# Two-layer graph kernel, one core: adj times h0 before W_g, scores in the wide product, 512-column E pieces, loops written out

## The reference, cut to what matters

```python
h0 = maximum(layernorm(x), 0)                        # x: 2048 x 256
h  = h0 @ W_sa;  s_left = h @ a_l;  s_right = h @ a_r
e  = where(adj != 0, exp(-leaky_relu(s_left[:, None] + s_right[None, :], 0.01)), 0)
x_a = (e / (sum(e, axis=1) + 1e-5)) @ h              # adj: 2048 x 2048, zeros and ones
x_b = adj @ (h0 @ W_g) + b_g
gate_a = sigmoid([adj @ h0, h0] @ Wa.T + ba);  gate_b = sigmoid([adj @ h0, h0] @ Wb.T + bb)
out = x + sigmoid(gate_a * x_a + gate_b * x_b)
```

## Time and profile before

| | us |
|---|---|
| median of 3 runs (190.56 to 190.69) | 190.69 |
| span of the profiled execution, first to last instruction | 189.2 |
| outside the span (the difference) | 1.5 |
| PE, DVE, ACT, POOL busy | 175.0, 154.3, 117.3, 37.1 |

### The profile page before, as it was taken

One profiled execution on the slowest core, in us unless ns is written; L12 is line 12 of the kernel. 1 busy time (PEld: TensorE's weight loads), 2 busy tenths in 40 slices (PEclk: granted clock), 3 DMA queues, 4 the chain that ended last, 5 costly groups with the idle time before them and its releaser, 6 DMA issues.

```text
span 189.2 us, 4431 instructions
## 1 busy us (share of the span) xinstructions
PE 175.0 (92%) x1576; PEld 144.4 (76%) x1576; DVE 154.3 (82%) x389; ACT 117.3 (62%) x231; POOL 37.1 (20%) x86
## 2 busy tenths in 40 slices
PE   0359899999999999999999999999999999999993
PEld 0335465466888888888888888888888888888892
DVE  0698789999999989996997898599869896997341
ACT  2197586899647958664696458466727764594310
POOL 1057770099970010002000200020020000000000
DMA  5920797000029008311901470175109210001100
GB/s 141 396 102 0 110 185 155 2 3 0 0 28 196 2 5 155 67 59 16 196 15 55 63 158 6 49 120 102 55 0 178 43 55 0 0 0 55 61 28 28
DMA packets 4621, 13.67 MB, mean 72 GB/s; under 512 B 512, under 2 KB 896, under 8 KB 4608
## 3 DMA queue, kind: packets, MB, share of 16 engines
q0 software_dynamic: 2304, 8.39, 24.8%
q1 hardware_dynamic: 2016, 4.20, 6.2%
q10 hardware_dynamic: 288, 0.92, 1.3%
HBM read 19.80 MB, written 2.10 MB: 116 GB/s over the span
## 4 chain that ended last, share of the span: by engine, by line
PE 80%; DVE 3%; issue 0%; ACT 0%; DVEq 0%
PE ps L800 15%; PE ps L801 15%; PE ps L807 14%; PE ps L808 14%; PE ps L806 14%; PE ps L765 4%; PE ps L838 1%; PE ps L837 1%; PE ps L836 1%; DVE mv_lo L603 1%; PE ps L756 1%; DVE h0t_lo L581 1%; DVE mv_lo L601 1%; PE ps L745 0%; DVE e_raw L342 0%; DVE far L333 0%
## 5 line engine op out<-in xcount | busy, mean ns | idle before, releaser
L349 ACT ACTIVATE e_raw<-e_raw,log_e 128x512 f32<-128x512 f32 x64 | 46.1, 720 | 43.9 <-DVE e_raw L342 43.1
L806 PE MATMUL ps<-mv_lo,e_hi 128*128 128x257 f16 x240 | 65.5, 273 | 0.0
L808 PE MATMUL ps<-mv_hi,e_lo 128*128 128x257 f16 x240 | 65.5, 273 | 0.0
L807 PE MATMUL ps<-mv_hi,e_hi 128*128 128x257 f16 x240 | 65.4, 272 | 0.0
L342 DVE SCALAR_TENSOR_TENSOR e_raw<-sl_row,exs,far 128x256 f32<-128x256 f16 (+1 forms) x128 | 56.6, 482 | 2.5 <-DVE far L333 2.0
L801 PE MATMUL ps<-mv_lo,adj 128*128 128x258 f16 x256 | 56.9, 272 | 0.0
L800 PE MATMUL ps<-mv_hi,adj 128*128 128x258 f16 x256 | 56.9, 273 | 0.0
L360 DVE TENSOR_TENSOR e_lo<-e_raw,e_hi 128x512 f16<-128x512 f32 x64 | 44.5, 697 | 3.8 <-ACT e_hi L356 3.8
L356 ACT ACTIVATE e_hi<-e_raw 128x512 f16<-128x512 f32 x64 | 39.3, 616 | 0.0
L800 PEld LDWEIGHTS ps<-mv_hi,adj 128*128 128x128 f16 x256 | 24.7, 96 | 3.8 <-ACT sl_row L471 0.2
L801 PEld LDWEIGHTS ps<-mv_lo,adj 128*128 128x128 f16 x256 | 24.8, 97 | 3.3
(11 more groups left out here) (80 smaller groups left out, 179.9 us busy)
## 6 DMA issues: line engine op xcount, KB each, us to landing
adj<-in_adj_t POOLq DMA_DIRECT2D x16, 512.0 KB, 7.1
x_sb<-in_x SPq DMA_DIRECT2D x4, 512.0 KB, 8.0
out<-res SPq DMA_DIRECT2D x7, 256.0 KB, 2.0
w_sb<-in_weights ACTq DMA_DIRECT2D x1, 512.0 KB, 8.1
c_sb<-in_consts ACTq DMA_DIRECT2D x1, 391.0 KB, 5.7
out<-res SPq DMA_DIRECT2D x1, 128.0 KB, 1.8
out<-res SPq DMA_DIRECT2D x2, 64.0 KB, 1.6
```

The costliest lines, as they stand in the source:

```text
L349: act.activation(e_raw[:, p % RING, :, :], e_raw[:, p % RING, :, :], ACT.Exp, bias=log_e[:, 0:1], scale=SLOPE - 1.0).then_inc(exp_done, 1)
L806: pe.matmul(a_bank(s, q), e_hi[:, j, cols], mv_lo[:, j, 0, 0:D + 1], start=(j == 0), stop=False)
L807: pe.matmul(a_bank(s, q), e_hi[:, j, cols], mv_hi[:, j, 0, 0:D + 1], start=False, stop=False)
L808: return pe.matmul(a_bank(s, q), e_lo[:, j, cols], mv_hi[:, j, 0, 0:D + 1], start=False, stop=(j == NT - 1))
```

## The change

- adj is no longer multiplied with h0 W_g, but with h0 itself: `b_products` (stationary the natural-layout parts nat_hi, nat_lo of h0, moving adj16 at 512 columns, two 128-row halves k of the result) gives the aggregate, transposed. `agg_highs` and `agg_lows` split it, and `post` multiplies it with W_g and the left gate vectors (258 columns, 6 matmuls a tile). There are now 4 chunks (c) of 512 rows, and 8 pairs of tiles (p).
- `narrow` is gone. The scores and the right gate vectors stand beside W_sa: `wide` has 260 columns.
- relu comes before the transpose (`h0_tiles`), and h0 is split twice: as it stands (`nat_highs`, `nat_lows`) and transposed (`h0t_highs`, `h0t_lows`). The transposes have one set of banks (0, 1), which `sl_rows` also writes; so `turn(g)` waits for the copy `sl_rows(g-2)` on ACT. `wide(g)` has four banks and waits for `mv_lows(g-1)`.
- The reciprocal square root is one pow on POOL; the Newton steps are gone.
- E comes in 32 pieces (n) of two adj tiles by 512 columns, all of them after the head, with a ring of 12 pieces for PE (ESLOT). Pair p waits for `a_side(p-2)` on DVE (a_read).
- adj has three slots, is loaded from the landing of x's second part on, in 9 loads. The weights' load waits for x's first part. The half that is added to x is now added on ACT.
- All engine programs are written out, without loops.

The core of the diff:

```diff
-CW = 256
+CW = 512
+ZRING = 3
+ESLOT = 12
+ADJ = 3
+WA = D + NX
+WG = D + 2
+WIDE_BANKS = (2, 3, 6, 7)
+B_BANKS = (4, 6, 4, 4)
+ADJ_PIECES = ((0, 0, 4), (0, 4, 8), (0, 8, 16), (1, 0, 8), (1, 8, 16), (2, 0, 8), (2, 8, 16), (3, 0, 8), (3, 8, 16))
...
         def _(pool):
-            def correct(g):
...
+            def norms(g):
+                ts = slice(g * GT, (g + 1) * GT)
+                pool.wait_ge(var_ready, g + 1)
+                pool.tensor_tensor(rstd[:, ts], var_s[:, ts], power[:, :], ALU.pow).then_inc(rstd_ready, 1)
+                pool.wait_ge(rstd_ready, g + 1)
+                pool.tensor_tensor(shift[:, ts], neg_mean[:, ts], rstd[:, ts], ALU.mult).then_inc(norm_ready, 1)
...
+            pool.wait_ge(x_landed[1], 16)
+            load_adj(0)
+            norms(0)
+            load_adj(1)
+            norms(1)
+            load_adj(2)
+            load_adj(3)
+            norms(2)
+            load_adj(4)
+            scales(0)
...
+            pool.wait_ge(b_done, 1)
+            pool.wait_ge(far_ready, JP)
+            load_adj(7)
+            load_adj(8)
...
         def _(act):
             act.dma_start(c_sb[:, :], consts).then_inc(c_landed, 16)
-            act.dma_start(w_sb[:, :, :, :], weights).then_inc(w_landed, 16)
+            act.wait_ge(x_landed[0], 16)
+            act.dma_start(w_sb[:, :, :], weights).then_inc(w_landed, 16)
...
+            h0_tiles(0)
             act.wait_ge(wl_product, 1)
             act.wait_ge(w_landed, 16)
+            act.activation(w_sb[:, :, D:D + 2], wl_bank, ACT.Copy).then_inc(wl_ready, 1)
+            act.wait_ge(wl_ready, 1)
+            act.activation(w_hi[:, :, 0:WA], w_sb[:, :, 0:WA], ACT.Copy, scale=W_SCALE).then_inc(w_high, 1)
+            h0t_highs(0)
+            nat_highs(0)
+            h0_tiles(1)
+            h0t_highs(1)
+            nat_highs(1)
             factors(0)
+            h0_tiles(2)
+            mv_highs(0)
+            sl_rows(0)
+            h0t_highs(2)
+            nat_highs(2)
+            factors(1)
+            h0_tiles(3)
+            mv_highs(1)
+            sl_rows(1)
+            h0t_highs(3)
...
+            def dve_far(n):
...
+                dve.tensor_scalar(far[:, n % 2, :, :], adj16[:, c % ADJ, j:j + 2, :], -FAR, FAR, ALU.mult, ALU.add)\
+            def dve_z(n):
...
+                if n >= ZRING:
+                    dve.wait_ge(e_ready, n - ZRING + 1)
...
+            dve_far(0)
+            for n in range(NE):
+                if n + 1 < NE:
+                    dve_far(n + 1)
+                dve_z(n)
+                if n >= LAG:
+                    dve_low(n - LAG)
...
+                if n == 20:
+                    agg_lows(3)
+                for p in range(2, 6):
+                    if n == 4 * p + 10:
+                        b_parts(p)
+                    if n == 4 * p + 11:
+                        b_gates(p)
+                    if n == 4 * p + 13:
+                        a_side(p)
+                    if n == 4 * p + 15:
+                        results(p, p)
...
+            def turn(g):
+                if g >= 1:
+                    pe.wait_ge(h0t_ready, g * KT)
+                if g >= 2:
+                    pe.wait_ge(sl_ready, g - 1)
...
+            def b_products(c, j0, j1):
+                if j0 == 0 and c == 1:
+                    pe.wait_ge(mv_ready, NT)
...
+                    for k in range(KT):
+                        for h in range(2):
+                            ins = pe.matmul(ps[:, B_BANKS[c] + k, :], nat[h][:, j, k * P:(k + 1) * P],
+                                            adj16[:, c % ADJ, j, :], start=(j == 0 and h == 0), stop=(j == NT - 1 and h == 1))
...
+            def a_pair(p):
...
+                if p >= 2:
+                    pe.wait_ge(a_read, p - 1)
+                for j in range(NT):
+                    if j % 2 == 0 and pr == 0:
+                        pe.wait_ge(e_ready, c * JP + j // 2 + 1)
...
+                    if j == NT - 1:
+                        ins.then_inc(a_done, 1)
+                    elif j % 2 == 1 and pr == 1:
+                        ins.then_inc(e_used, 1)
+                    if j == NT // 2:
+                        post(p)
...
             turn(0)
+            wide(0)
             turn(1)
+            b_products(0, 0, 4)
+            wide(1)
+            sl_rows(0)
             turn(2)
+            b_products(0, 4, 8)
+            wide(2)
+            sl_rows(1)
             turn(3)
+            b_products(0, 8, 12)
+            wide(3)
+            sl_rows(2)
+            b_products(0, 12, 16)
+            sl_rows(3)
+            b_products(1, 0, 16)
+            b_products(2, 0, 16)
+            a_pair(0)
+            a_pair(1)
+            b_products(3, 0, 16)
+            for p in range(2, NPAIR - 1):
+                a_pair(p)
+            last_pair()
```

More of the change, by code:

```diff
@@ L467, in sl_rows @@
[L467 to L479 removed]
+                for t in range(g * GT, (g + 1) * GT):
+                    act.activation(mv_hi[:, t, 0:D], ps[:, WIDE_BANKS[t % GT], 0:D], ACT.Copy,
+                                   scale=scale_a[:, t:t + 1]).then_inc(mv_high, 1)
@@ L706, in _ @@
[L706 to L713 removed]
+            h0t_lows(2)
@@ new lines, in _ @@
+            for n in range(NE - LAG, NE):
+                dve_low(n)
+            for p in range(2, 6):
+                if 4 * p + 10 >= NE:
+                    b_parts(p)
+                if 4 * p + 11 >= NE:
+                    b_gates(p)
+                if 4 * p + 13 >= NE:
+                    a_side(p)
+                if 4 * p + 15 >= NE:
+                    results(p, p)
+            b_parts(6)
+            b_gates(6)
+            a_side(6)
+            results(6, 6)
+            b_parts(7)
@@ new lines, in wide @@
+            def wide(g):
+                pe.wait_ge(h0t_ready, (g + 1) * KT)
+                if g == 0:
+                    pe.wait_ge(w_ready, 1)
+                    pe.wait_ge(wl_ready, 1)
+                for t in range(GT):
+                    if g:
+                        pe.wait_ge(mv_ready, g * GT + t - GT + 1)
+                    for i, (k, a, b) in enumerate(three):
+                        ins = pe.matmul(ps[:, WIDE_BANKS[t], 0:WA], h0t[a][:, g % 2, k, t * P:(t + 1) * P],
+                                        w2[b][:, k, 0:WA], start=(i == 0), stop=(i == len(three) - 1))
+                    ins.then_inc(wide_product, 1)
@@ new lines, in post @@
+            def post(p):
+                c, pr = p // 2, p % 2
+                if p == 0:
+                    pe.wait_ge(w_ready, 2)
+                    pe.wait_ge(agg_ready, 2)
+                else:
+                    pe.wait_ge(b_read, p)
+                    pe.wait_ge(agg_ready, c + 1)
+                for q in range(2):
+                    cols = slice((2 * pr + q) * P, (2 * pr + q + 1) * P)
+                    for i, (k, a, b) in enumerate(three):
+                        ins = pe.matmul(ps[:, 6 + q, 0:WG], agg[a][:, c % AGG, k, cols], w2[b][:, k, WA:WA + WG],
+                                        start=(i == 0), stop=(i == len(three) - 1))
+                ins.then_inc(post_product, 1)
@@ L760, in wide @@
-            def wide(g, half):
-                for t in range(g * GT + 2 * half, g * GT + 2 * half + 2):
-                    if t >= WB:
-                        pe.wait_ge(wide_ready, t - WB + 1)
-                    for i, (k, a, b) in enumerate(three):
-                        ins = pe.matmul(wide_bank(t), h0t[a][:, k, t * P:(t + 1) * P],
-                                        (w_hi, w_lo)[b][:, k, :, :], start=(i == 0), stop=(i == len(three) - 1))
-                    ins.then_inc(wide_product, 1)
```

980 lines of the change are left out of this document (419 added, 561 removed).

## The result

The changed kernel takes **194.27 us** (median of 4 runs, 194.11 to 194.71) against 190.69 (190.56 to 190.71 in the same job): the ratio is 1.0189, 95% interval 1.0177 to 1.0202. So it is slower by 3.6 us; 1.1 was forecast. The direction held, and so did the stated range (189.0 to 195.2); the size did not, and the forecast's own range, 190.5 to 193.3, was left by 1.0 us. The profiled execution has a span of 192.6 us, 1.7 less than the median.

What follows compares the result with a forecast made beforehand. PE's stage-two work behind a head was taken as the bound: head 50.1, then 140.2 to the span's end, plus 1.5 from span to median, gives 191.8 us. Its own range was 190.5 to 193.3, the stated one 189.0 to 195.2.

Steps and rivals of the forecast that it cites:

- Stage two: PE's work after the head, without waits: 136.8 us against 141.0 before, a saving of 4.2.
- Tb: Start of b_products(1), where the head ends: forecast at 50.1 us, against 44.78 before.
- The ring of ACT and PE: In the head, turn, wide and sl_rows wait in turn with ACT's work; one cycle takes 10.2 us.
- a round: One cycle in the head from a turn's start to the next: 10.2 us, with two PE waits.
- the start: Head up to the start of wide(0): forecast at 13.8 us, with w landed at 11.0.
- later than 12: Sign of being wrong: ACT's w_hi in the head coming after 12 us; it was forecast at 11.2.
- the last part: End of the head, from turn(3) at 38.35 to b_products(1) at 50.1: 11.75 us.
- the clock: PE's clock level during wide(0): 2.7 us at the upper, 5.2 at the lower; 4.15 taken, between.
- the head begins sooner: Rival: wide(0) at the upper clock level (-1.45), w landed by 10.5 (-0.4), cheaper copies: 189.7 us, chance 0.22.
- DVE late: Rival: in stage two DVE comes late to a_side(4), which pair 6 waits for: 194.3 us, chance 0.27.
- the late first group: Rival: at the head's start w lands at 14.3 or the first pow is slow: 192.3 to 195.1, chance 0.10.
- The margin to pair 6: In stage two DVE ends a_side(4) at Tb + 112.6, PE arrives at Tb + 112.9: 0.3 us to spare.

Runs made afterwards that it cites:

- the kernel with the new order: Changed kernel with the same head operations reordered on ACT, DVE and POOL (h0 tiles, mv_highs and mv_lows earlier), PE's order untouched: 190.28 us, ratio 0.9983.
- The exchange on DVE: Changed kernel with mv_lows(2) put ahead of nat_lows(3) on DVE, for the last group only: 193.56 us, ratio 1.0136.
- the kernel with norms first: Changed kernel with POOL's norms(0) ahead of the wait for x's second part and the first adj load: 194.28 us, ratio 1.0172.
- fillers: Changed kernel with eight more transposes, into a bank nobody reads, on PE between turn(0) and wide(0): 192.48 us, ratio 1.0081.
- the added operations: Changed kernel with the eight extra transposes, plus two one-column DVE operations in each E step: 193.45 us, ratio 1.0142.

## Why the prediction was wrong in its size

**The mechanism held.** Stage two got shorter (Tb to the end 139.9, against 144.4 from 44.78 before; 140.2 was forecast, a gain of 4.2, and 4.5 came). The head got longer by more (Tb from 44.78 to 52.66, 7.9; 5.3 forecast). The ring of ACT and PE bounds the head, a round is 10.3 (10.2 forecast) with PE's two waits of 1.79 and 0.73 (1.9 and 0.8), and PE never waits behind Tb. That the ring is the cause was only argued in the prediction; the kernel with the new order shows it, 3.9 us from the order alone.

**Mis-sized: the start**, 13.8 for 15.09. The sentence "The first h0 tiles end at about 11 too, since xn did at 11.03 with a chain as long" took the new chain for as long as the old. It isn't: the tiles end at 12.33, since POOL stands behind x's second load and the issue of an adj load (8.15 to 8.86), and the pow is 1.05. With it w_hi, at 12.42, is "later than 12", one of the prediction's own signs of being wrong. The price was in the text, as a rival with 0.10 ("a pow of 1.1 adds 0.5"), where it belonged in the sum. In size it was right by luck: the row of 1099 ns is a multiply held by DVE (below), and no pow. That row and the rows of 0.2 are ends of a range, and for an operation never seen the low one was used. The place behind the load wasn't counted at all, though the diff has it; it is 0.35 of the 1.29. But pow and its place hold `wide(0)` by only 0.5 beyond w. The other 0.8 is a second term of the same sum, covered by the first: w, taken at 11.0, is issued at 6.50 and takes 5.2, so it lands at 11.7, and with `wide(0)` 2.9 behind it (11.4 and 14.30 in the kernel without pow) the start would have been 14.6. Its row on the page of the changed kernel is

```profile
w_sb<-in_weights ACTq DMA_DIRECT2D x1, 518.0 KB, 5.2
```

**Mis-sized: the last part**, 11.75 for 12.65. The step "nat_lows on DVE holds mv_lows(2) until 3.7" named DVE's nat_low as what ends last. It ends 3.3 behind ACT's start, but the same nat_low holds POOL's scale_a until then, and only behind that can ACT begin mv_highs(2); `wide(3)` starts at 4.54. The exchange on DVE takes 0.84 of that away. The prediction had named no price for scale_a on this path. The trace of before showed the same thing: the 1099 ns in the earlier trace rows belong to an operation that began at 37.54, beside DVE's z (37.04) and low (37.83), which read two operands from SBUF as nat_low does; the prediction had it as "one takes 1.1".

**Right, but by luck in its middle: the clock.** `wide(0)` was put at 4.15, between 2.7 and 5.2, and took 4.32, 5.18 in the kernel with norms first, and 2.69 with fillers. A value between two levels is no forecast of one execution; the two ends were. The rival "the head begins sooner" (-1.45 for the upper level) had the price right; its cause was within reach of a change of two lines.

**Right, but by luck: the stated range.** 194.3 lies in 189.0 to 195.2 only because the range was stretched for rivals. One of them, DVE late, was put at 194.3, but it didn't happen; the other, the late first group (192.3 to 195.1), did happen, but with 1.3 it gives 193.1 and not 194.3.

**Right:** unrolling at 0 (1.0004). By the Trainium skill (Runtime: NRT & Kernel Launch, section Instruction fetch mechanics) there is a stall where a taken branch leaves the prefetched stretch. At PE's back edge the trace shows none, and the time shows none to win back on any engine; whether these branches leave the stretch isn't shown. The Trainium skill (GPSIMD Engine Reference, section 2.1 Instruction dispatch) has some 6 us for the first call of a freshly loaded library kernel. That doesn't bear on pow: the first one starts 0.03 behind the issue ahead of it (8.86 and 8.89) and is as long as the second, 1.05 and 1.04. **DVE's step** was forecast at 2.8 and is 2.79 in the changed kernel (its timeline, a mask to the next mask: 68.30 to 71.09):

```profile
68.30 0.42 DVE L488 TENSOR_SCALAR scratch<-adj 128x1024 f16<-128x1024 f16 x1
68.63 1.41 DVE L499 SCALAR_TENSOR_TENSOR scratch<-sl_row,exs,scratch 128x512 f32<-128x512 f32 x2
69.96 1.22 DVE L507 TENSOR_TENSOR e_lo<-scratch,e_hi 128x1024 f16<-128x1024 f32 x1
71.09 0.42 DVE L488 TENSOR_SCALAR scratch<-adj 128x1024 f16<-128x1024 f16 x1
```

The margin to pair 6 was 0.7 to 0.8 rather than 0.3. The rival that hung on it, with 0.27, was rightly the less likely one, but the added operations show that it was near: some 0.07 more a step, 0.8 / 11, would have reached it.

## What to carry to other kernels

Work that is moved from a stage in which an engine never waits into one where it waits in turn with another engine costs its full time there, unless the order in that ring is made for it; look at the new cycle's length, not at the sums of work. Price an operation that the trace doesn't show with a range from the cheap row to the dear one, ask why the dear row is dear, and follow every wait ahead of it in its queue. A term that is covered by another has to be right as well: w was as wrong as pow, and showed only when pow was gone. And where PE stands idle ahead of its first dense stretch of matmuls, try to fill the gap: that was worth 1.8 us here.

## What the runs showed of the hardware

**POOL is held by DVE.** A POOL operation on four columns takes 0.21 to 0.26 us, and 1.05 if DVE is in a `tensor_tensor` of 1024 columns with both inputs in SBUF: it ends when that does (22.55 + 1.22 = 23.77 on DVE, 22.81 + 1.06 = 23.87 on POOL). Three kernels tell it apart from other causes: without pow on POOL it stays (1.06), after 9.04 us of idleness it isn't there (0.22), and moving the one DVE operation takes it away for that group alone (0.21). The Trainium skill (SBUF — State Buffer, section SBUF: two separate sides) says that the two engines share a port pair, which a DVE operation with two SBUF inputs locks for its whole duration against a POOL operation that reads SBUF; the rows at 22.55 and 22.81 agree. DVE's h0t_low, with one input in PSUM, ran from 30.49 to 31.78 in the kernel with the ring's new order, and scale_a, at 31.22, took 0.22 beside it.

**A pow of four columns takes POOL 1.03 to 1.05 us**, with DVE at rest too (18.35 in the changed kernel); a multiply of the same shape, 0.20. Beside DVE's w_lo, which reads two operands from SBUF, one took 1.46 (at 13.06 in the kernel with the ring's new order).

**The clock at the first dense matmuls** depends on what PE did just before: behind 2.0 us of idleness `wide(0)` ran at the lower level (0.217 for 260 columns, 1.2 GHz) for 3.4 us of its 4.3, in the execution with norms first for all of 5.2; with the gap filled it ran at the upper (0.11, 2.4 GHz), though in one execution only after 1.5 us. The windows' clock column reads 1.00 over this stretch all the same (also from 15.10 to 18.40 alone), so the start times are what to read. The times don't show that filling the gap makes a kernel steadier: the executions of kernels that left it lie 0.4 to 1.5 us apart, those of kernels that filled it 0.15, 0.45, 0.9 and 1.0. Which executions rise early, and why, stays open.
